# Attention and experts on one core: the second maximum item behind one round with V, routing in four places, and down's product ahead of gate and up

## The chip, the cores and the metric

One core of a Trainium2 chip runs the whole program. The metric is the device time of one execution in microseconds (us), the median of the runs. The engines are PE (TensorE; PEld is its weight loading), ACT (ScalarE), DVE (VectorE), POOL (GpSimd) and SP (SyncE, which issues DMAs here). Each works its own queue in the order of the program and meets the others by semaphores.

## The reference

Two layers over x of shape (2, 2048, 128), float32, each with a residual and a layer norm:

```python
# attention: 16 query heads, 4 key/value heads of 8, window of 128 to either side
Q = (x @ Wq.T).reshape(B, S, HKV, G, HEAD_DIM); K, V likewise from Wk, Wv
scores = einsum('bskgd,bswkd->bskgw', Q, K_win) * scale   # w: 257 places around s, -inf outside
out = einsum('bskgw,bswkd->bskgd', softmax(scores), V_win).reshape(...) @ Wo.T
x = layernorm(x + out)
# experts: 8, the best 2 of softmax(x @ router); their weights through a softmax again
down = (silu(x @ gating[e]) * (x @ up[e])) @ down[e]       # D 128, F 256
x = layernorm(x + sum over the two experts of weight * down)
```

## The kernel before

**Attention.** The 4096 tokens are 32 tiles of 128. Step s (from -2) works on three tiles at once, in five items each: the maximum items A0 to A4 of tile s+2 (`a_item`, matmuls L715, L719, L727, L730, whose maxima DVE takes in `largest_score`, L1328 and L1332), the probability items B0 to B4 of tile s (`b_item`, L754, L745, L766; ACT makes their exponentials, L1056), and V for tile s-1 in rounds of up to two items (`values(t, n)`, L790: round 0 at the end of step t, rounds 1 and 2 early in step t+1). Items use three pairs of PSUM banks in turn, in the order A0 B0 A1 B1 A2 B2 A3 B3 A4 B4, so an item waits until the one three places ahead of it is read (`wait_pair`). The rest of a step on PE: `maxima` (L796), the turned row tile for the router (`turn`, L814), `sums` (L803, of the copy `po` that ACT makes of V's result), in some steps a projection (L848, L850, L841), `logits` (L819) or `ranks` (L828, L831), and `output` (L809). DVE's step is the five reductions, with the reciprocal (L1375) and `attT` (L1378) between the third and the fourth, the residual (L1390) and its statistics (L1397). In between stand the routing operations: `rt_op` (21 for eight tiles: the two best experts and their weights) at three places of a step by `RT_AT`, `slot_op` (8: the row of the expert's region to which a token goes) in one piece by `SLOT_AT`, and `table_op` (19: which block of rows belongs to which expert) by `TABLE_0` and `TABLE_AT`. POOL makes the norm (`norm`, 12 small operations, then x1, L629) and writes the rows sorted by expert to memory (`sort_rows`, L647).

**Experts.** 44 units k of two blocks of 128 rows, in three parts: units 0 to 19 (tiles 0 to 15), 20 to 35 (16 to 27), 36 to 43 (28 to 31). A unit goes through `turn_rows` (PE, transposes of its rows, L945), `round_rows` (ACT, xh, L1111), `rest_rows` (DVE, xl, L1415), `gate_up` (PE, two value loads from the table, which give the expert's column, then six matmuls, L962 to L964), `silu` (ACT, L1118), `hidden` (DVE, L1421), `turn_hidden` (PE, L973), `hidden_out` (ACT, copy from PSUM, L1124), `down` (PE, L982) and `rows_made` (ACT, copy L1130 and the DMA to ys, L1133). The engines' loops over k:

```python
# PE: the steps of MOE_STEPS, then        # ACT: the steps, then
turn_rows(k + 1)                          round_rows(k + 1)
gate_up(k)        # waits xl_done k+1     silu(k)            # waits g_psum k+1
turn_hidden(k-1)  # waits h_done k        hidden_out(k-1)    # waits hT_psum k
down(k-2)         # waits hT_done k-1     rows_made(k-2)     # waits d_psum k-1
```

`turn_rows(k+1)` waits for the rows' DMA and for `xl_done` k+1, that is for `rest_rows(k)`. Steps 32 to 45 (the end of the last tile's attention, its norm, and the last tiles' routing) are put in between: `MOE_STEPS` gives step 32 to unit 0, 33 to 1, 34 to 3, 35 to 4 and so on to 45 in unit 14.

**The end.** POOL gathers each token's two result rows (`rows_back`, L659, 64 gathers in one row of work). Those of a part start when all ys of that part are written (`rows_done`). DVE adds them to x1 (`combine`, L1433) and takes the norm's factors for sets of tiles (`SETS`), ACT scales (L1138), SP writes the output.

Of the kernel before, what the change touches and what calls it, by code (L numbers as in the profile page):

```python
# [10 lines left out]
I32 = mybir.dt.int32  # L11
# [9 lines left out]
NT = TOK // P  # L21
# [38 lines left out]

SETS = [(0, TPS)] + [(t, t + 4) for t in range(TPS, NT, 4)]
CB_TILE, CB_SET = 4, 12
# [11 lines left out]
def part_of(t):  # L74
    return next(ph for ph, (a, b) in enumerate(PARTS) if a <= t < b)
# [121 lines left out]

RT_AT, RANK_AT, SLOT_AT = {}, {}, {}
for m_ in range(NT // RT_TILES):
    s_ = 8 * m_ + 15  # L200
    if m_ < NT // RT_TILES - 2:
        RT_AT.update({s_: (m_, (0, 2), (2, 4), (4, 6)), s_ + 1: (m_, (6, 11), (11, 12), (12, 13)),
                      s_ + 2: (m_, (13, 18), (18, 20), (20, 21))})
        RANK_AT[s_ + 2] = m_
        SLOT_AT[s_ + 3] = m_
    else:
        last_ = m_ == NT // RT_TILES - 1
        RT_AT.update({s_: (m_, (0, 2), (2, 2), (2, 2)), s_ + 1: (m_, (2, 7), (7, 7), (7, 7)),
                      s_ + 2: (m_, (7, 12), (12, 12), (12, 12)), s_ + 3: (m_, (12, 18), (18, 18), (18, 18)),
                      s_ + 4: (m_, (18, 21), (21, 21), (21, 21))} if last_ else  # L210
                     {s_: (m_, (0, 2), (2, 9), (9, 18)), s_ + 1: (m_, (18, 18), (18, 21), (21, 21))})
        RANK_AT[s_ + 1 + 3 * last_] = m_
        SLOT_AT[s_ + 2 + 3 * last_] = m_
RANK_AT[8 * (NT // RT_TILES) + 12] = len(RANKED) - 1
SLOT_AT[8 * (NT // RT_TILES) + 13] = len(RANKED) - 1

# [38 lines left out]
def attention_moe(nc, x, xT, wq, wk, wv, wo, wr, wgu, wd, consts, out, q_scr, xs, ys):  # L255
    with ExitStack() as ctx:
# [193 lines left out]
        def _(sp):  # L450
# [38 lines left out]
            def step(s):  # L489
# [21 lines left out]
                if s in (15, 17, 19):  # L511
                    zeros_last((s - 15) // 2)
                if s == 27:
                    zeros_behind(0, 0, E)
# [45 lines left out]
        def _(pool):  # L560
# [102 lines left out]
            def step(s):  # L663
                if projected(s) is not None:
                    project(*projected(s))
                if s == 28:
                    for t in range(12, 16):
# [7 lines left out]
                if s == 27:  # L675
                    for t in range(8, 12):
                        sort_rows(t)
# [3 lines left out]
            for k in range(NU):  # L681
                if k in MOE_STEPS:
                    step(MOE_STEPS[k])
                if 2 <= k < 10:
                    sort_rows(14 + k)
                if 14 <= k < 18:
                    sort_rows(2 * k - 4)
                    sort_rows(2 * k - 3)
            for t in range(NT):
# [3 lines left out]
        def _(pe):  # L693
# [172 lines left out]
            def step(s):  # L866
# [21 lines left out]

                a_item(s + 2, 1)
                b_item(s, 1)  # L890
# [97 lines left out]
            for k in range(NU):  # L988
                if k in MOE_STEPS:
                    step(MOE_STEPS[k])  # L990
# [12 lines left out]
        def _(act):  # L1003
# [138 lines left out]
            for k in range(NU):  # L1142
                if k in MOE_STEPS:
                    step(MOE_STEPS[k])
# [7 lines left out]
                if k and k in MOE_STEPS:  # L1152
                    routing_exps(MOE_STEPS[k])
            hidden_out(NU - 1)
# [6 lines left out]
        def _(dve):  # L1161
# [174 lines left out]
            def negated(t):  # L1336
                parts = 1 if last_of_batch(t) else 2
                dve.wait_ge(a_max, COUNT["A", t, a_items(t)[-1]])
                if t >= 2:
# [3 lines left out]
                                  AX.X, ALU.max, negate=True).then_inc(nm_done, 1)  # L1343

            def step(s):
                t, a = s - 1, s + 2
                m, *ops = RT_AT.get(s, (0, (0, 0), (0, 0), (0, 0)))
# [4 lines left out]
                if s in SLOT_AT:  # L1352
                    for n in range(SL_OPS):
                        slot_op(SLOT_AT[s], n)
                for n in range(*TABLE_0.get(s, (0, 0))):
                    if s < 30:
                        table_op(0, n)
                g = ln_group(s)
                if g is not None:
                    y = nw[:, g % 2, 1, :]  # L1360
                    dve.wait_ge(mv_done, 4 * g + 4)
                    if g >= 2:
                        dve.wait_ge(x1_done, 4 * (g - 1))
                    dve.tensor_scalar(nw[:, g % 2, 0, :], mv[:, g % 2, :, 1], EPS, None, ALU.add).then_inc(ln_seed, 1)
                    dve.wait_ge(ln_seed, 2 * g + 1)
                    dve.tensor_scalar(y.bitcast(I32), nw[:, g % 2, 0, :].bitcast(I32), -0.5, float(RSQRT_SEED),
                                      ALU.mult, ALU.add).then_inc(ln_seed, 1)
                for n in range(*ops[0]):
                    rt_op(m, n)
                largest_score(a, 1)  # L1370
                largest_score(a, 2)
                if 0 <= t < NT:
                    dve.wait_ge(nd_psum, t + 1)
                    wait(dve, att_done, t)
                    dve.reciprocal(rden[:], pV[:, P:2 * P]).then_inc(den_done, 1)  # L1375
                    dve.wait_ge(den_done, t + 1)
                    wait(dve, y_psum, t)
                    dve.tensor_tensor(attT[:], pV[:, 0:P], rden[:], ALU.mult).then_inc(att_done, 1)  # L1378
                largest_score(a, 3)
                largest_score(a, 4)  # L1380
                if 0 <= a < NT:
                    negated(a)
                for n in range(*TABLE_0.get(s, (0, 0))):
                    if s >= 30:
                        table_op(0, n)
# [5 lines left out]
                for n in range(*ops[1]):  # L1391
                    rt_op(m, n)
                if 0 <= t < NT:
# [4 lines left out]
                for n in range(*ops[2]):  # L1398
                    rt_op(m, n)

# [62 lines left out]
            for k in range(NU):  # L1463
                if k == 0:
                    step(MOE_STEPS[k])
                if k + 1 < NU:
                    rest_rows(k + 1)
                hidden(k)
                if k and k in MOE_STEPS:
                    step(MOE_STEPS[k])  # L1470
# [89 lines left out]
```

## Time and profile before

| | |
|---|---|
| median of three runs | 575.82 us (570.12 to 578.64) |
| profiled execution | 575.41 us, its span 573.8 us |
| mean granted clock of PE | 0.924 |
| busy, share of the span | PE 483.0 us, 84%; PEld 52%; DVE 363.3 us, 63%; ACT 301.1 us, 52%; POOL 241.3 us, 42% |
| attention, steps to the last reciprocal but one | until about 368 us |
| expert units, gate's first matmul of unit 0 to down of unit 43 | 375.7 to 543.8 us |
| last gather issued, end of the span | 562.9 and 573.8 us |

A span is the time from the first to the last instruction; about 1.6 us of the execution lie around it. A matmul's end is modelled. In a timeline line, what stands in brackets is how long the engine was idle before it, and what released it; "issue" is time for which the profile shows no wait. A matmul of 512 columns in the experts' part (L962 to L964) takes 0.39 us in the records at full clock and 0.63 at the lower.

### The profile page before, as it was taken

How to read it: one execution, taken by the hardware profiler on the slowest of the kernel's cores; microseconds unless marked ns; L12 is line 12 of the kernel's file. 1: busy time of each engine (PE TensorE's matmuls, PEld its weight loads, DVE VectorE, ACT ScalarE, POOL GpSimd, SP SyncE). 2: the span in 40 equal slices, each digit the busy share in tenths (PEclk: the TensorE clock that was granted, in tenths of full speed). 3: DMA queues.
4: the chain of work that ended last, by engine and by line, in shares of the span. 5: the costliest groups of instructions: out<-in, count | busy, mean ns of one | idle time of the engine just before them, and what ended most of it. 6: DMA issues, size and time to landing. Idle time of an engine off the chain costs nothing.

```text
span 573.8 us, 12084 instructions
## 1 busy us (share of the span) xinstructions
PE 483.0 (84%) x3865; PEld 296.8 (52%) x3865; DVE 363.3 (63%) x825; ACT 301.1 (52%) x516; POOL 241.3 (42%) x329
## 2 busy tenths in 40 slices
PE   4399899899999999999998988977978899999700
PEld 3264345445454454445454444456867788888500
DVE  1366567778676496668688677652354645677784
ACT  2125455566556455466566466732575555555462
POOL 2131051752532232232746763007701727754772
PEclk9999798999999797799999799967998999999955
DMA  6343116126207225215205130111421445542362
GB/s 164 58 75 72 29 48 149 29 49 148 40 12 174 40 66 121 34 43 121 53 18 83 54 88 21 39 46 47 133 79 54 138 141 159 135 124 71 91 168 59
DMA packets 83948, 46.93 MB, mean 82 GB/s; under 512 B 40496, under 2 KB 79408, under 8 KB 83120
## 3 DMA queue, kind: packets, MB, share of 16 engines
q1 hardware_dynamic: 65216, 31.04, 24.4%
q0 software_dynamic: 4096, 8.40, 5.4%
q10 hardware_dynamic: 14576, 6.72, 4.3%
q8 instruction: 34, 0.56, 0.4%
q14 instruction: 26, 0.21, 0.1%
HBM read 26.47 MB, written 19.40 MB: 80 GB/s over the span
## 4 chain that ended last, share of the span: by engine, by line
PE 57%; DVE 17%; issue 10%; DMA 6%; SPq 3%; POOL 3%; ACT 3%; ACTq 0%; POOLq 0%; DVEq 0%
PE pV L790 12%; DVE mp L1328 7%; PE pX L982 6%; PE pX L962 5%; PE pX L715 5%; PE pX L964 4%; PE pX L963 4%; DMA xt<-xT 3%; DVE rden L1375 3%; PE pX L754 3%; PE pV L973 3%; PE pM L809 2%; PE pX L766 2%; PE pX L745 2%; SPq L435 2%
## 5 line engine op out<-in xcount | busy, mean ns | idle before, releaser
L1328 DVE TENSOR_REDUCE mp<-pX 128x4 f32<-128x1024 f32 (+4 forms) x128 | 149.1, 1187 | 84.4 <-PE pX L719 68.2
L1056 ACT ACTIVATE probs<-pX 128x1024 f32<-128x1024 f32 x152 | 152.6, 1023 | 91.3 <-PE pX L745 75.9
L790 PE MATMUL pV<-probs,vx 128*32 128x512 f32 (+1 forms) x736 | 90.7, 591 | 0.0
L647 POOL DMA_INDIRECT xs<-xr,slot x64 | 63.0, 985 | 44.6 <-DVE ends L1248 26.2
L659 POOL DMA_INDIRECT probs<-ys,source x64 | 64.0, 1001 | 38.1 <-issue 35.4
L715 PE MATMUL pX<-kx,q 48*128 48x512 f32 (+4 forms) x256 | 61.4, 479 | 9.4 <-DMA q<-q_scr 9.4
L754 PE MATMUL pX<-q,kx 50*128 50x512 f32 x248 | 63.0, 505 | 2.5 <-DVE mp L1328 2.0
L1421 DVE TENSOR_TENSOR probs<-probs,pX 128x512 f32<-128x512 f32 x44 | 30.3, 688 | 43.0 <-ACT probs L1118 43.0
L715 PEld LDWEIGHTS pX<-kx,q 48*128 48x128 f32 x256 | 26.2, 203 | 47.7 <-issue 36.1
L962 PE MATMUL pX<-we,qh 128*128 x88 | 41.0, 466 | 11.6 <-issue 9.5
L982 PE MATMUL pX<-we,probs 128*128 x352 | 47.6, 279 | 0.7 <-ACT vx L1130 0.7
L1118 ACT ACTIVATE probs<-pX 128x512 f32<-128x512 f32 x44 | 26.3, 597 | 37.4 <-PE pX L964 37.4
L982 PEld LDWEIGHTS pX<-we,probs 128*128 128x128 f32 x352 | 43.6, 195 | 1.0 <-issue 1.0
L586 POOL CAST kh<-ks 128x512 fp32r<-128x512 f32 x7 | 4.3, 610 | 81.5 <-ACT ks L1033 81.5
L963 PE MATMUL pX<-we,qh 128*128 x88 | 36.5, 415 | 0.0
L964 PE MATMUL pX<-we,ql 128*128 x88 | 36.4, 413 | 0.0
L1415 DVE TENSOR_TENSOR ql<-pX,qh 128x256 fp32r<-128x256 f32 x44 | 18.6, 422 | 26.4 <-ACT qh L1111 25.0
L754 PEld LDWEIGHTS pX<-q,kx 50*128 50x128 f32 x248 | 25.8, 205 | 15.5 <-issue 7.9
L599 POOL CAST qh<-qs 128x512 fp32r<-128x512 f32 x7 | 4.3, 610 | 69.9 <-ACT qs L1036 69.9
L1375 DVE RECIPROCAL rden<-pV 128x128 f32<-128x128 f32 x32 | 30.3, 948 | 4.8 <-PE pV L803 4.8
L790 PEld LDWEIGHTS pV<-probs,vx 128*32 128x32 f32 x736 | 18.0, 114 | 27.5 <-issue 21.4
L745 PE MATMUL pX<-mask 64*128 64x256 bf16 (+1 forms) x184 | 31.9, 343 | 0.0
(151 smaller groups left out, 832.5 us busy)
## 6 DMA issues: line engine op xcount, KB each, us to landing
q<-q_scr SPq DMA_DIRECT2D x46, 128.0 KB, 4.3
xt<-xs SPq DMA_DIRECT2D x88, 64.0 KB
ys<-vx ACTq DMA_DIRECT2D x44, 128.0 KB, 1.9
xt<-xT SPq DMA_DIRECT2D x8, 512.0 KB, 5.9
q_scr<-qh SPq DMA_DIRECT2D x32, 64.0 KB
q<-stage SPq DMA_DIRECT2D x128, 2.0 KB
xr<-x SPq DMA_DIRECT2D x8, 256.0 KB, 6.4
raw<-wgu SPq DMA_DIRECT2D x4, 512.0 KB, 5.7
```

Source lines behind the costliest of these rows:

```text
L647: pool.indirect_dma_start(xs[ph][:, :], bass.IndirectOffsetOnAxis(ap=slot[:, t, k:k + 1], axis=0), tile(t), None, bounds_check=ROWS - 1, o ...
L659: pool.indirect_dma_start(yin[:, t % YIN, k, :], None, ys[ph][:, :], bass.IndirectOffsetOnAxis(ap=source[:, t, k:k + 1], axis=0), bounds_c ...
L715: mm = pe.matmul(bank[:, pr, 0:64 * (k1 - k0)], q_cols(t, KA, pr, i, i + 1), k_cols(KA, pr, k0, k1), start=True, stop=True, skip_group_che ...
L754: mm = pe.matmul(bank[:, pr, :], k_cols(KB, pr, k0, k0 + 2), q_cols(t, KB, pr, 0, 4), start=True, stop=True, skip_group_check=True)
L790: mm = pe.matmul(pV[row:row + 32, cols], vx[:, chunk, pr, :], src[:, pr, cols], start=n == 0, stop=True, skip_group_check=True)
L962: pe.matmul(to, xh[:, k % 2, rows], hi, start=True, stop=False, skip_group_check=True)
L963: pe.matmul(to, xh[:, k % 2, rows], lo, start=False, stop=False, skip_group_check=True)
L964: mm = pe.matmul(to, xl[:, k % 2, rows], hi, start=False, stop=True, skip_group_check=True)
L982: mm = pe.matmul(pX[2][:, 1, h * D:(h + 1) * D], hidT[:, k % 2, at:at + P], we[:].bitcast(F32)[:, bass.ds(expert[k, h] + 4 * F + f * D, D) ...
L1056: act.activation(dst, src[:], ACT.Exp).then_inc(exp_done, 1)
L1328: dve.tensor_reduce(mp[:, t % 2, 0, :, i, :], src[:, :, 0:2 * n].rearrange("p r (c v k) -> p r v c k", v=NV, k=32), AX.XY, ALU.max).then_i ...
L1375: dve.reciprocal(rden[:], pV[:, P:2 * P]).then_inc(den_done, 1)
```

## The change

On PE, A1 goes ahead of V's round 2 and of the maxima. Routing and slot operations are spread over four places of DVE's step, slots over two steps, and the norm's seeds of step 33 stand ahead of them. Steps 34 and 35 go to unit 4, 36 and 37 to unit 5, 38 to 45 to units 6 to 13. Rank matmuls, sorts and tables are shifted to fit. In a unit `down(k-2)` stands ahead of `gate_up(k)` on PE and `rows_made(k-2)` ahead of `silu(k)` on ACT. In DVE's step `seeds(g)` and `routing(place)` are helpers around the old operations. `combine` starts one unit sooner, and the first set for the last norm has 20 tiles instead of 16.

```diff
-SETS = [(0, TPS)] + [(t, t + 4) for t in range(TPS, NT, 4)]
+SETS = [(0, 20), (20, 24), (24, 28), (28, 32)]
...
     if m_ < NT // RT_TILES - 2:
-        RT_AT.update({s_: (m_, (0, 2), (2, 4), (4, 6)), s_ + 1: (m_, (6, 11), (11, 12), (12, 13)),
-                      s_ + 2: (m_, (13, 18), (18, 20), (20, 21))})
-        RANK_AT[s_ + 2] = m_
-        SLOT_AT[s_ + 3] = m_
+        RT_AT.update({s_: (m_, (0, 2), (2, 2), (2, 2), (2, 5)), s_ + 1: (m_, (5, 7), (7, 8), (8, 11), (11, 13)),
+                      s_ + 2: (m_, (13, 15), (15, 15), (15, 18), (18, 21))})
+        RANK_AT[s_ + 3] = m_
+        SLOTS_AT.update({s_ + 3: (m_, (0, 0), (0, 0), (0, 0), (0, 3)), s_ + 4: (m_, (3, 5), (5, 6), (6, 8), (8, 8))})
...
-        TABLE_0 = {27: (0, 5), 30: (5, 13), 31: (13, TB_OPS)}
+        TABLE_0 = {30: (0, 9), 31: (9, TB_OPS)}
...
-        TABLE_AT = (14, 18)
+        TABLE_AT = (13, 18)
...
-            COMBINE_AT.append(max([LAST_UNIT[part_of(t)] + 6] + [n + 1 for n in COMBINE_AT[-1:]]))
-        MOE_STEPS = {k: NT + i for i, k in enumerate((0, 1, 3, 4, 5, 6, 7, 8, 9, 10, 11, 12, 13, 14))}
+            COMBINE_AT.append(max([LAST_UNIT[part_of(t)] + 5] + [n + 1 for n in COMBINE_AT[-1:]]))
+        MOE_STEPS = {0: [NT], 1: [NT + 1], 4: [NT + 2, NT + 3], 5: [NT + 4, NT + 5]}
+        MOE_STEPS.update({k: [NT + k] for k in range(6, 14)})
...
@@ -873,7 +874,10 @@
                 if has(s - 1):
-                    for n in range(1, len(rounds(s - 1))):
+                    values(s - 1, 1)
+                a_item(s + 2, 1)
+                if has(s - 1):
+                    for n in range(2, len(rounds(s - 1))):
                         values(s - 1, n)
...
-                a_item(s + 2, 1)
                 b_item(s, 1)
                 a_item(s + 2, 2)
...
@@ -986,15 +989,15 @@
                     turn_rows(k + 1)
+                if k >= 2:
+                    down(k - 2)
                 if k:
                     gate_up(k)
                     turn_hidden(k - 1)
-                if k >= 2:
-                    down(k - 2)
...
@@ -1140,17 +1143,17 @@
                     round_rows(k + 1)
+                if k >= 2:
+                    rows_made(k - 2)
                 silu(k)
                 if k:
                     hidden_out(k - 1)
-                if k >= 2:
-                    rows_made(k - 2)
...
@@ -1342,32 +1345,40 @@
+                if g is not None and s > NT:
+                    seeds(g)
+                routing(0)
                 largest_score(a, 1)
+                if g is not None and s <= NT:
+                    seeds(g)
+                routing(1)
                 largest_score(a, 2)
...
                     dve.tensor_tensor(attT[:], pV[:, 0:P], rden[:], ALU.mult).then_inc(att_done, 1)
+                routing(2)
                 largest_score(a, 3)
...
                     dve.bn_stats(st6[:, t % 4, :], tile(t)).then_inc(st_done, 1)
+                routing(3)
```

## Rows read from the trace of the kernel before

**Rows 1.** timeline, steps 6 and 7: start us, us, engine, line, operation [idle before <-releaser]
```profile
104.90 1.50 PE L790 MATMUL pV<-probs,vx 128*32 128x512 f32 x16
...
106.72 0.49 PE L715 MATMUL pX<-kx,q 48*128 48x512 f32 x2
...
107.30 2.36 DVE L1328 TENSOR_REDUCE mp<-pX 128x4 f32<-128x1024 f32 x2 [1.42 <-PE pX L719]
...
107.65 0.21 PE L719 MATMUL pX<-mask 64*128 64x64 bf16 x2
...
109.57 0.95 DVE L1375 RECIPROCAL rden<-pV 128x128 f32<-128x128 f32 x1
...
112.03 0.50 PE L766 MATMUL pX<-q,kx 50*128 50x256 f32 x4 [1.08 <-DVE mp L1328]
...
119.71 0.95 DVE L1375 RECIPROCAL rden<-pV 128x128 f32<-128x128 f32 x1
```
**Rows 2.** waits over the whole span: us in total, times, longest us
```profile
PE pX L962 <- issue: 9.5, 19, 1.1
...
PE pX L766 <- DVE mp L1328: 8.2, 17, 1.1
```
**Rows 3.** busy time by stretch: PE, PEld, DVE, ACT, POOL, granted clock, DMA, GB/s
```profile
461.10:527.00 65.90, 64.06 (x409) 54.56 (x408) 41.51 (x116) 37.13 (x82) 36.34 (x37) 1.00 0.46 126
...
394.00:401.00 7.00, 7.00 (x30) 6.27 (x30) 1.11 (x2) 2.00 (x5) 5.62 (x7) 0.51 0.21 60
```
**Rows 4.** timeline, expert unit 37
```profile
516.05 0.49 PE L962 MATMUL pX<-we,qh 128*128 x1
...
517.99 1.06 PE L982 MATMUL pX<-we,probs 128*128 x8
...
518.24 0.58 ACT L1124 COPY probs<-pV 128x512 f32<-128x512 f32 x1
...
518.88 0.38 PE L945 MATMUL pX<-cst,xt 128*128 128x128 f32 x2
```
**Rows 5.** timeline, expert unit 16
```profile
445.31 0.41 DVE L1415 TENSOR_TENSOR ql<-pX,qh 128x256 fp32r<-128x256 f32 x1
...
445.88 0.41 PE L945 MATMUL pX<-cst,xt 128*128 128x128 f32 x2
...
447.42 0.49 PE L962 MATMUL pX<-we,qh 128*128 x1 [1.14 <-issue]
```
**Rows 6.** timeline, expert units 23 and 24
```profile
471.19 0.49 PE L962 MATMUL pX<-we,qh 128*128 x1 [0.23 <-issue]
...
472.05 0.42 DVE L1415 TENSOR_TENSOR ql<-pX,qh 128x256 fp32r<-128x256 f32 x1 [1.28 <-ACT qh L1111]
...
474.15 0.50 PE L962 MATMUL pX<-we,qh 128*128 x1
```
**Rows 7.** timeline, GpSimd's gathers: first of the last 32, of the last 8
```profile
522.36 0.99 POOL L659 DMA_INDIRECT probs<-ys,source  x1 [9.90 <-issue]
...
553.75 1.00 POOL L659 DMA_INDIRECT probs<-ys,source  x1 [0.30 <-issue]
```
**Rows 8.** timeline, expert unit 43: gate's first matmul and down's last eight
```profile
537.18 0.50 PE L962 MATMUL pX<-we,qh 128*128 x1
...
542.64 1.15 PE L982 MATMUL pX<-we,probs 128*128 x8 [0.65 <-ACT vx L1130]
```
**Rows 9.** timeline, expert units 2 and 3
```profile
385.89 0.58 ACT L1124 COPY probs<-pV 128x512 f32<-128x512 f32 x1 [0.26 <-PE pV L973]
...
385.93 0.78 PE L962 MATMUL pX<-we,qh 128*128 x1
...
392.89 0.30 PE L814 MATMUL pM<-cst,xr 128*128 128x128 f32 x1 [3.43 <-POOL xr L629]
```
**Rows 10.** timeline, expert unit 12, at the lower clock
```profile
431.60 0.79 PE L962 MATMUL pX<-we,qh 128*128 x1 [1.14 <-issue]
...
435.27 0.58 ACT L1124 COPY probs<-pV 128x512 f32<-128x512 f32 x1
```

More of the change, by code:

```diff
@@ L512, in step @@
                     zeros_last((s - 15) // 2)
-                if s == 27:
+                if s == 28:
                     zeros_behind(0, 0, E)
@@ L666, in step @@
                 if s == 28:
-                    for t in range(12, 16):
+                    for t in range(8, 12):
                         sort_rows(t)
@@ L674, in step @@
                     sort_rows(s - 20)
-                if s == 27:
-                    for t in range(8, 12):
+                if s == 29:
+                    for t in range(12, 16):
                         sort_rows(t)
@@ L681, in _ @@
             for k in range(NU):
-                if k in MOE_STEPS:
-                    step(MOE_STEPS[k])
+                for s in MOE_STEPS.get(k, ()):
+                    step(s)
                 if 2 <= k < 10:
                     sort_rows(14 + k)
-                if 14 <= k < 18:
-                    sort_rows(2 * k - 4)
-                    sort_rows(2 * k - 3)
+                if 13 <= k < 17:
+                    sort_rows(2 * k - 2)
+                    sort_rows(2 * k - 1)
             for t in range(NT):
@@ L988, in _ @@
             for k in range(NU):
-                if k in MOE_STEPS:
-                    step(MOE_STEPS[k])
+                for s in MOE_STEPS.get(k, ()):
+                    step(s)
                 if k + 1 < NU:
                     turn_rows(k + 1)
+                if k >= 2:
+                    down(k - 2)
                 if k:
@@ L1142, in _ @@
             for k in range(NU):
-                if k in MOE_STEPS:
-                    step(MOE_STEPS[k])
+                for s in MOE_STEPS.get(k, ()):
+                    step(s)
                 if k + 1 < NU:
                     round_rows(k + 1)
+                if k >= 2:
+                    rows_made(k - 2)
                 silu(k)
@@ L1149, in _ @@
                     hidden_out(k - 1)
-                if k >= 2:
-                    rows_made(k - 2)
-                if k and k in MOE_STEPS:
-                    routing_exps(MOE_STEPS[k])
+                    for s in MOE_STEPS.get(k, ()):
+                        routing_exps(s)
             hidden_out(NU - 1)
@@ L1343, in negated, with seeds, routing @@
                                   AX.X, ALU.max, negate=True).then_inc(nm_done, 1)
+            def seeds(g):
+                y = nw[:, g % 2, 1, :]
+                dve.wait_ge(mv_done, 4 * g + 4)
+                if g >= 2:
+                    dve.wait_ge(x1_done, 4 * (g - 1))
+                dve.tensor_scalar(nw[:, g % 2, 0, :], mv[:, g % 2, :, 1], EPS, None, ALU.add).then_inc(ln_seed, 1)
+                dve.wait_ge(ln_seed, 2 * g + 1)
+                dve.tensor_scalar(y.bitcast(I32), nw[:, g % 2, 0, :].bitcast(I32), -0.5, float(RSQRT_SEED),
+                                  ALU.mult, ALU.add).then_inc(ln_seed, 1)
             def step(s):
                 t, a = s - 1, s + 2
-                m, *ops = RT_AT.get(s, (0, (0, 0), (0, 0), (0, 0)))
+                nothing = (0, (0, 0), (0, 0), (0, 0), (0, 0))
+                m, *ops = RT_AT.get(s, nothing)
+                r, *ranked = SLOTS_AT.get(s, nothing)
+                def routing(place):
+                    for n in range(*ops[place]):
+                        rt_op(m, n)
+                    for n in range(*ranked[place]):
+                        slot_op(r, n)
+                g = ln_group(s)
                 largest_score(a, 0)
@@ L1351, in step @@
                     dve.bn_aggr(mv[:, ((t - 1) // 4) % 2, (t - 1) % 4, :], st6[:, (t - 1) % 4, :]).then_inc(mv_done, 1)
[L1352 to L1369, printed above, removed]
+                if g is not None and s > NT:
+                    seeds(g)
+                routing(0)
                 largest_score(a, 1)
+                if g is not None and s <= NT:
+                    seeds(g)
+                routing(1)
                 largest_score(a, 2)
@@ L1390, in step @@
                     dve.tensor_tensor(tile(t), pM[:, 256:384], tile(t), ALU.add).then_inc(z_done, 1)
-                for n in range(*ops[1]):
-                    rt_op(m, n)
-                if 0 <= t < NT:
                     if t >= 4:
@@ L1397, in step @@
                     dve.bn_stats(st6[:, t % 4, :], tile(t)).then_inc(st_done, 1)
-                for n in range(*ops[2]):
-                    rt_op(m, n)
+                routing(3)
             dve.wait_ge(q_split, 1)
@@ L1464, in _ @@
                 if k == 0:
-                    step(MOE_STEPS[k])
+                    step(NT)
                 if k + 1 < NU:
@@ L1468, in _ @@
                 hidden(k)
-                if k and k in MOE_STEPS:
-                    step(MOE_STEPS[k])
+                if k:
+                    for s in MOE_STEPS.get(k, ()):
+                        step(s)
                 for ph in range(1, NPH):
```

21 lines of the change are left out of this document (10 added, 11 removed).

## The prediction

> **What bounds the kernel now.** I read the page first: PE is busy 84% of a span of 573.8 us (the page's table above), and no other engine reaches 64%. A share is an average, so each stage was then read by itself in the timeline.
>
> *Attention, 32 steps.* A settled step lasts 10.13 us: one reciprocal starts at 109.57, the next at 119.71 [rows 1]. It is one loop through two engines. PE lands the second maximum item (L715 at 106.72), DVE reduces it and the third (2.36 us), takes the reciprocal, reduces the fourth; only then may PE start the last probability item (L766, behind a wait of 1.08 us for DVE). From there PE runs on through V's round 0, the next step's first items, V's rounds 1 and 2 and the maxima, and lands the next second item. Steps that also carry a projection or logits use that slack: over all steps L766 waits for DVE only 8.2 us [rows 2].
>
> *Experts, 44 units of two blocks.* From 461.1 to 527 PE is busy 64.06 of 65.9 us at the full granted clock [rows 3]. PE's order in unit k is rows turned for k+1 (T), gate and up of k (G), hidden turned for k-1 (H), down of k-2 (D). In unit 37 G starts at 516.05, D at 517.99, T at 518.88 [rows 4]. From G of unit 24 at 474.15 to that of unit 37 the mean unit is 41.9 / 13 = 3.22 us, and 2.96 us, G of unit 23 at 471.19 to G of unit 24 at 474.15, is PE's own work without a gap [rows 6]. The rest comes with the pair of value loads in front of G, which are instructions of PE's queue. In unit 16 DVE finishes xl at 445.31 + 0.41 = 445.72, T starts at 445.88, and G only at 447.42: 1.54 us from T to G on an empty array, 1.70 us from xl [rows 5]. I formed this distance for all units from 2 to 43: it is never under 1.66 us and in half of them within 0.1 us of that. Units 23 and 24 show it again: 472.05 + 0.42 = 472.47 to 474.15 is 1.68 us [rows 6]. So PE's queue doesn't reach the value loads while T's wait for xl is open, and from its release to G there is a fixed 1.7 us.
>
> *The end.* GpSimd gathers 64 times in a row, 1.30 us each. The last 32 start at 522.36, when the result of unit 35 is in memory; the eight of the last part, from 553.75 on, need unit 43 [rows 7]. Unit 43's D starts at 542.64 [rows 8], some 7 us before it is needed. So today unit 35 sets the end, and the units behind it are covered by the gathers.
>
> **The change, part by part.**
>
> *Second maximum item ahead of V's last round.* It moves A1 ahead of V's round 2 and the maxima. Rounds 1 and 2, maxima and x1's turn take 104.90 to 106.72, 1.82 us together; round 2 and the two small ones are about 1.1 us of it [rows 1]. DVE then reduces A1 in its present idle time, and the chain starts from the third item instead, which lands where it did. Before, DVE began the third reduction when half of 2.36 us was over, at 108.48; the item had landed with L719's end, 107.65 + 0.21 = 107.86. So the loop shortens by 0.62 us, to about 9.5 us. Where PE's own work is the bound (projections, logits), only the present wait of L766 can be won, 0.2 to 0.3 us. Five steps (2, 6, 25, 27, 28) have the full wait: 5 x 0.62 = 3.1 us; the others bring what is left of the 8.2 us, some 2.9 us. Sum 6.0 us. V's round 2, the copy of the output and the maxima end 0.4 to 0.5 us later; the copy's follower (sums) stands behind A2 anyway.
>
> *Routing in four places.* The same operations of about 0.2 us. Some now stand between A1 and A2 and behind the reciprocal, on DVE's chain, three or four per step in some six steps: 0 to 3 us; I take 1. Attention together: -5 us (-9 to -1).
>
> *Later units for steps 34 to 37, seeds first.* PE stood 3.43 us in unit 3 for GpSimd's norm (L814 at 392.89) [rows 9]. A unit later this wait is gone. It is not booked separately: below, units are counted at their new length, which replaces it.
>
> *D ahead of G, result copy ahead of SiLU.* Here is the cost. D(k-2) needs the copy of hidden rows of k-2 (L1124). That copy needs H(k-2), which stands at the end of unit k-1, and on ACT it stands behind SiLU(k-1), which needs G(k-1). Before, a whole unit lay between copy and D. Now only T does. In unit 37 G starts at 516.05 and the copy ends at 518.24 + 0.58 = 518.82: 2.77 us behind G's start [rows 4], the same in every unit at full clock. D cannot start sooner, and behind D in PE's queue stand the value loads for G(k). So a unit costs 2.77 us, then the release to G. With T in between that release costs 1.68; with D's eight matmuls instead of T's two, somewhat more. Bound: G of unit 23 starts at 471.19 behind a gap, and by 472.47 PE's queue has already passed 6 + 4 + 8 matmuls [rows 6], 1.28 us or at most 0.07 each, so six more cost at most 0.43. A unit is between 2.77 + 1.66 = 4.43 and 2.77 + 1.68 + 0.43 = 4.88 us. I take 4.7, against 3.22 now. ACT and DVE have about 2.0 and 1.4 us of work in a unit and don't bind.
>
> *Extras of early units.* Unit 4 carries steps 34 and 35: logits wait for x1T's copy, which stands behind the hidden copy on ACT, +1.6; unit 5 +0.5; the second logits +0.3; the two exponentials with table loads between SiLUs +2.9. Together 5.3 us (2 to 8).
>
> *Combine one unit sooner, sets of 20.* Twelve operations of 0.2 us leave the tail of DVE; they lie beside gathers: 0.
>
> **The sum**, against the profiled run (span 573.8, 1.6 around it: 575.4; the median of the three is 575.8). G of unit 2 starts at 385.93. Attention takes 5 off; D(0) waits for the copy that ends at 385.89 + 0.58 = 386.47 [rows 9], so G(2) moves to 386.47 + 1.68 + 0.25 = 388.4, less 5 is 383.4. 41 units at 4.7 are 192.7, extras 5.3: G(43) starts at 581.4. From G(43) to D(43) is 542.64 - 537.18 = 5.46 [rows 8]: 586.9. From D(35) at 517.99 to the gather at 522.36 are 4.37 [rows 4, 7]: the last eight gathers start at 591.2. Unit 35 would let them start sooner: G(36) at 548.5, D(35) at 551.5, gathers from 555.9, 24 x 1.30 later is 587.1. So the end passes from GpSimd to PE. From the first of the eight gathers to the end of the span is 573.8 - 553.75 = 20.05: 611.3, and with 1.6 around it **613 us**.
>
> One rule of the Trainium skill speaks against this working. The page Perfetto Trace Analysis, section Per-engine timelines, has a matmul wait in a queue of its own while the sequencer already decodes what follows; by it the value loads would run while D waits. The trace does not agree for T's wait (never under 1.66 us); whether it holds for D's no row shows. By the rule it would be rival 1.
>
> **Rivals.**
>
> 1. *D's wait holds back D, not the value loads.* Then a unit is 2.77, 0.24 (as from the copy to D at the end) and D's 0.89 (517.99 to 518.88, where T follows): 3.9 us. G(2) 382.6, G(36) 520.5, D(35) 523.5, gathers from 527.9, and 51.4 us more: 579.3, **581 us**. For it: some waits may travel with their matmul. Against: rows 5 and 6.
>
> 2. *The granted clock falls in the new gaps.* PE would work 2.96 of 4.7 us. At the lower level (1.2 GHz) unit 12 had 4.25 us from G to the end of the copy (431.60 to 435.27 + 0.58) [rows 10], against 2.77: +1.5 us a unit, **674 us** if all 41 ran so, 643 for half. For it: after PE's 3.43 us of standing, 394 to 401 ran at 0.51 [rows 3, 9]. Against: the new gaps are each near 1 us, and unit 16 with its 1.14 us stayed at full clock [rows 5].
>
> 3. *Faster: the value loads' 9.5 us of idle time before G [rows 2] vanish and D finds its copy ready.* With it 3.4 us of the norm wait, 5 of attention, 2 as D(35) comes earlier in its unit: 575.4 - 19.9 = **555 us**. It decides where the copy ends before T does, within about 2.0 us of G's start; the rows say 2.77, and nothing in the change brings SiLU or H forward. Only if ACT's copy needed no H could it be.
>
> **Chances.** Forecast (unit of 4.4 to 4.9 us, clock mostly full) 0.67, its own range 597 to 622; rival 1 and mixtures with it (575 to 597) 0.12; rival 2 (622 to 674) 0.16; rival 3 0.05. The range 588 to 640 takes in the bounds of the unit's length (41 x 0.27 down, 41 x 0.18 up), of attention and extras, part of rival 1 and the half of rival 2, and leaves out some 0.2. Two per cent, about what can be told from no change here, is 564 to 587: faster 0.05, within 0.07, slower 0.88.
>
> **What the profile would show.** Right: steps of 9.5 us where no projection is, 9.9 otherwise; no 3.4 us wait at L814; in the units D directly behind T, starting 0.05 to 0.25 us behind the end of L1124; about 0.8 us of PE idle before L982 and 1 us or more before L962; unit length 4.7; the last eight gathers waiting for ys. Wrong: D starting within 2 us of G (the reading of the order is false), or no idle before L962 (rival 1), or L962 at 0.63 us instead of 0.40 through the units (rival 2).

## The result and the profile after

The changed kernel takes 639.61 us, median of four runs (630.02 to 645.32); the kernel before, on the same chip, 573.88 us (570.12 to 578.64). The ratio is 1.107, with a 95% interval of 1.098 to 1.117. Here and below a ratio isn't that of the medians, because every kernel has quicker and slower executions and only the quicker are compared (630.02 and 636.78 us of the four here); one execution of a later kernel, which took 670.2 us at a mean granted clock of 0.62, is left out in the same way. The profiled execution is the quickest of the four, 630.02 us with a span of 628.4, so the sum of 613 us, made against one profiled execution, is to be held against 630.0 first, and the median stands another 9.6 us above it.

TensorE now stands still for a part of every unit. The two rows that carry this in the page of the changed kernel are PE's busy tenths in 40 slices and the granted clock beside them:

```profile
PE   3599999999989799899998977776777777776720
...
PEclk8559899999999879999968895999999999999965
```

From slice 26 on PE is at 7 where the kernel before had 9, and the clock did not fall. The windows of the changed kernel (columns as in rows 3) put a number on it:

```profile
450.00:500.00 50.00, 36.03 (x209) 28.62 (x208) 19.94 (x66) 17.31 (x41) 22.20 (x23) 1.00 0.39 111
500.00:550.00 50.00, 35.54 (x208) 28.14 (x207) 21.00 (x58) 18.49 (x43) 25.39 (x26) 1.00 0.34 88
```

PE is busy 36.0 and 35.5 of 50 us at a granted clock of 1.00, against 64.06 of 65.9 before [rows 3]. Two units of the changed kernel, PE's timeline and then ScalarE's (line numbers are three higher than before in these functions: gate and up L965 to L967, hidden turned L976, rows turned L948, down L985, hidden copy L1127):

```profile
473.97 0.49 PE L965 MATMUL pX<-we,qh 128*128 x1 [0.76 <-issue]
...
475.46 0.60 PE L976 MATMUL pV<-cst,probs 128*128 128x128 f32 x4
475.89 0.38 PE L948 MATMUL pX<-cst,xt 128*128 128x128 f32 x2
476.87 1.15 PE L985 MATMUL pX<-we,probs 128*128 x8 [0.59 <-ACT probs L1127]
478.77 0.49 PE L965 MATMUL pX<-we,qh 128*128 x1 [0.75 <-DVE ql L1422]
```
```profile
475.66 0.60 ACT L1121 ACTIVATE probs<-pX 128x512 f32<-128x512 f32 x1 [2.04 <-PE pX L967]
476.15 0.58 ACT L1127 COPY probs<-pV 128x512 f32<-128x512 f32 x1
```

This is the chain of the prediction, read off (G is the start of gate and up, D of down, T of the turned rows, as there): G starts at 473.97, the copy ends at 476.15 + 0.58 = 476.73, 2.76 us later (rows 4 had 2.77), D starts 0.14 us behind it, and the next G at 478.77, 1.90 us behind D. The unit is 4.80 us; over units 5 to 42 it is 4.80 to 4.96 and 4.86 in the mean, save two of 5.36 that carry later steps.

The waits of the changed kernel's TensorE (us in total, times, longest), which answer to rows 2:

```profile
PE pX L985 <- ACT probs L1127: 23.3, 39, 0.9
PE pX L965 <- DVE ql L1422: 22.5, 28, 0.9
PE pX L965 <- issue: 12.6, 16, 0.9
...
PE pX L767 <- DVE mp L1331: 7.3, 8, 1.8
...
PE pX L948 <- DMA xt<-xs: 3.9, 1, 3.9
```

Two gaps a unit, one before D (23.3 us) and one before G (22.5 + 12.6 = 35.1 us), where before there was one of 9.5 us [rows 2]. The gap before G is put down to DVE's ql for most units, though the ql that G needs has long been done: T, which stands ahead of D, waits for the same one (`xl_done` k+1), and the ql that ends shortly before G is the next unit's. Wherever it ends, G follows D by 1.83 to 2.06 us in all units from 2 on. It is the value loads, as the experiments show. The 3.9 us for unit 0's rows is new, and was not in the prediction. (L948 and L767 are three and one higher than L945 and L766 before.)

### The profile page after: what moved, and what is told of

It reads as the page before. It is cut to its first block, busy times and chain, and to the rows that moved or that the text cites. A ratio compares the mean times of both kernels' runs of the same rounds, so it can differ in the third digit from the quotient of the medians.

```text
span 628.4 us, 12072 instructions
## 1 busy us (share of the span) xinstructions
PE 494.0 (79%) x3865; PEld 293.2 (47%) x3865; DVE 364.6 (58%) x813; ACT 295.4 (47%) x516; POOL 241.8 (38%) x329
## 3 DMA queue, kind: packets, MB, share of 16 engines
q1 hardware_dynamic: 65216, 31.04, 22.5%
## 4 chain that ended last, share of the span: by engine, by line
PE 51%; DVE 17%; issue 12%; ACT 8%; DMA 7%; SPq 4%; POOL 1%; ACTq 0%; DVEq 0%; POOLq 0%
PE pV L791 12%; PE pX L965 5%; PE pX L716 5%; DMA xt<-xT 4%; PE pX L755 4%; DVE xr L1440 4%; PE pX L967 3%; PE pX L966 3%; ACT probs L1121 3%; PE pX L985 2%; ACT probs L1059 2%; DVE mp L1331 2%; PE pM L810 2%; SPq L435 2%; DVE ql L1422 2%
## 5 line engine op out<-in xcount | busy, mean ns | idle before, releaser
L1331 DVE TENSOR_REDUCE mp<-pX 128x4 f32<-128x1024 f32 (+4 forms) x128 | 151.7, 1189 | 81.0 <-PE pX L720 65.0
L791 PE MATMUL pV<-probs,vx 128*32 128x512 f32 (+1 forms) x736 | 95.0, 587 | 0.0
L985 PE MATMUL pX<-we,probs 128*128 x352 | 50.7, 287 | 23.9 <-ACT probs L1127 23.3
L965 PE MATMUL pX<-we,qh 128*128 x88 | 40.2, 457 | 35.1 <-DVE ql L1422 22.5
L985 PEld LDWEIGHTS pX<-we,probs 128*128 128x128 f32 x352 | 42.8, 191 | 33.5 <-issue 33.4
L965 PEld LDWEIGHTS pX<-we,qh 128*128 128x128 f32 x88 | 16.9, 192 | 45.8 <-issue 43.7
L1133 ACT COPY vx<-pX 128x256 f32<-128x256 f32 x44 | 16.4, 373 | 42.6 <-PE pX L985 42.6
L966 PE MATMUL pX<-we,qh 128*128 x88 | 35.6, 405 | 0.0
L967 PE MATMUL pX<-we,ql 128*128 x88 | 35.5, 403 | 0.0
L1066 ACT COPY po<-pV 128x512 f32<-128x512 f32 x32 | 18.8, 586 | 33.4 <-PE pV L791 33.4
```

Of the source, the lines that this page charges most:

```text
L791: mm = pe.matmul(pV[row:row + 32, cols], vx[:, chunk, pr, :], src[:, pr, cols], start=n == 0, stop=True, skip_group_check=True)
L965: pe.matmul(to, xh[:, k % 2, rows], hi, start=True, stop=False, skip_group_check=True)
L966: pe.matmul(to, xh[:, k % 2, rows], lo, start=False, stop=False, skip_group_check=True)
L967: mm = pe.matmul(to, xl[:, k % 2, rows], hi, start=False, stop=True, skip_group_check=True)
L985: mm = pe.matmul(pX[2][:, 1, h * D:(h + 1) * D], hidT[:, k % 2, at:at + P], we[:].bitcast(F32)[:, bass.ds(expert[k, h] + 4 * F + f * D, D) ...
L1331: dve.tensor_reduce(mp[:, t % 2, 0, :, i, :], src[:, :, 0:2 * n].rearrange("p r (c v k) -> p r v c k", v=NV, k=32), AX.XY, ALU.max).then_i ...
```

## The experiments

Each ratio is to runs of the kernel before on the same chip. The runs fell on four chips, which the text names where it matters.

**The order alone.** The kernel before with only the two orders moved:

```diff
-                if k:
-                    gate_up(k)
-                    turn_hidden(k - 1)
                 if k >= 2:
                     down(k - 2)
+                if k:
+                    gate_up(k)
+                    turn_hidden(k - 1)
```

and rows_made(k - 2) ahead of silu(k) on ScalarE.

> The kernel before with one part of the change alone: down(k-2) ahead of gate_up(k) on PE, rows_made(k-2) ahead of silu(k) on ACT. Theory (down waits for the copy of its hidden rows, and the value loads wait behind down): units of 4.8 to 4.95 us from unit 2 on, the end set by unit 43, 618 to 632 us, so nearly all of the changed kernel's loss. Rival (much of the loss is in attention, the start of the experts or the later steps of routing): units shorter than that and under 600 us.

Measured: 625.4 us against 574.0, ratio 1.097 (1.086 to 1.108). Its settled units are 4.80 to 4.96 us. The order of down is nine tenths of the loss by the ratios. Counted in the profiles from G of unit 0 to the end of the span, which leaves attention out, it is all of it: 198.1 us before, 254.2 with the order alone, 249.2 with the whole change.

**The order undone**, everything else of the change kept (the reverse of that diff).

> The changed kernel with that one part undone on both engines; all the rest of the change stays. Theory: units back to a mean of 3.2 us, the end again set by unit 35 and the gathers, 565 to 578 us; what the rest of the change brings or costs can be read from it. By my prediction's terms for attention (-5) and for the norm wait (-3.4) it would be 566 us; if the wait for the rows of unit 0 (3.85 us) and the half-clock stretches at the end of attention belong to the change, about 573. Rival (the rest costs as well): over 585.

Measured: 582.4 us, ratio 1.013 (1.005 to 1.022), with settled units of 3.0 to 3.5 us, 3.21 in the mean of units 24 to 37. From G of unit 0 to the end it takes 199.6 us, as the kernel before. So the rest of the change doesn't pay for itself either: a gain was expected, and it costs about one per cent here, ahead of the units. The experiments on attention below look into that.

**The value loads ahead of down's wait**, all else as in the changed kernel:

```diff
+            def loads(k):      # tb_ops wait and the two value loads, taken out of gate_up
...
+                if k:
+                    loads(k)
                 if k >= 2:
                     down(k - 2)
...
                 if k:
                     gate_up(k)
```

> The changed kernel with the two value loads of unit k ahead of down(k-2) instead of behind it; nothing else differs. Theory (the loads are held up behind down's wait): a unit is 2.77 to the copy's end, 0.14 to down, 0.9 of down and little more, 3.9 to 4.0 us, and the time falls to 585 to 597 us. Rival (the loads cost nothing, down or ACT's order is what lengthens the unit): still 4.8 us and 630 us.

Measured: 598.8 us, ratio 1.050 (1.034 to 1.067). The medians differ from the changed kernel's by 41 us, the profiled spans by 35 (593.5 against 628.4), and as much from G of unit 2 to G of unit 43 (167.2 against 202.2), with nothing else moved. PE's timeline of this kernel, one unit:

```profile
498.85 1.16 PE L989 MATMUL pX<-we,probs 128*128 x8 [0.60 <-ACT probs L1133]
499.76 0.48 PE L969 MATMUL pX<-we,qh 128*128 x1
...
502.66 1.15 PE L989 MATMUL pX<-we,probs 128*128 x8 [0.60 <-ACT probs L1133]
503.57 0.48 PE L969 MATMUL pX<-we,qh 128*128 x1
```

The wait before D is what it was (0.60 us); the one before G is gone, and G follows D by 0.91 us instead of 1.90. The unit is 3.81 us, which is rival 1's 3.9. So the loss of 1.64 us a unit (3.22 to 4.86) splits: 1.05 us is the loads standing bare behind the wait, and 0.59 us remains when they do not.

**The same loads moved in the kernel before**, a unit ahead:

```diff
...
+                if k == 0:
+                    loads(1)
                 if k:
                     gate_up(k)
+                    if k + 1 < NU:
+                        loads(k + 1)
                     turn_hidden(k - 1)
```

> The kernel before with the value loads of unit k+1 right behind gate_up(k), a unit ahead. Theory (before, 1.5 us of loads stand between the turned rows and gate and up, in a loop of two units of 6.5 us): the idle time before gate's first matmul falls from 9.5 us to near 0, units of 2.95 to 3.05 us, gathers of the second part 7 to 9 us sooner, 565 to 569 us. Rival (the loads are hidden today, PE is the bound): no change, 572 to 576 us.

Measured: 560.0 us, ratio 0.982 (0.970 to 0.995), and again on another chip, as the base of two later runs:

> The kernel before with the loads of unit k+1 behind gate_up(k), the same kernel as the fourth run, here as the base for the next two. Again 0.975 to 0.99 of before on a chip whose code arrives in time (units of 2.96 us); on one with long stalls of all engines, as in the last four runs, nearer 0.99.

Measured: 560.2 us against 572.0, ratio 0.976 (0.970 to 0.983). The windows of the first of the two:

```profile
460.00:500.00 40.00, 40.00 (x269) 35.42 (x269) 28.16 (x75) 24.29 (x55) 30.13 (x31) 1.00 0.57 152
```

PE busy 40.00 of 40 us, and units of 2.96 us, which is PE's own work [rows 6]. This is the quickest kernel of the study, and quicker than the 565 to 569 us expected.

**Twice as many value loads** in the changed kernel, to have their price by itself:

```diff
+                    pe.value_load(tab[0:1, ph, 1, i:i + 1], min_val=0, max_val=(E - 1) * EW)
                     expert[k, h] = pe.value_load(tab[0:1, ph, 1, i:i + 1], min_val=0, max_val=(E - 1) * EW)
```

> The changed kernel with each unit's two value loads issued twice (the first result of each pair is dropped), still behind the wait of down; nothing else differs. It measures the disputed price itself. Theory (TensorE issues nothing behind a wait, so the loads lie bare between down and gate_up): the changed kernel's units of 4.86 us and the 3.81 us of the kernel with the loads ahead put two loads at 1.05 us, so units of 5.7 to 6.1 us, the whole 670 to 690 us. Rival (most of the 1.05 us is something else, register moves or a refill behind the wait): units of 5.0 to 5.3 us, 640 to 655 us.

Its whole time, 810.1 us, can't be read against the changed kernel's: this run fell on a chip on which the kernel before takes 695.9 us. The unit can. PE's timeline at full clock:

```profile
569.97 1.15 PE L986 MATMUL pX<-we,probs 128*128 x8 [0.59 <-ACT probs L1128]
573.43 0.49 PE L966 MATMUL pX<-we,qh 128*128 x1 [2.31 <-issue]
```

The idle time before G is 2.31 us, not 0.75: two loads more cost 1.56 us, and the unit is 6.37 us (567.06 to 573.43), above both theories' figures. (Every third unit or so of this run falls to the lower clock and takes 7.8 us.) The wait before D is again 0.59. So a pair of loads takes about 1.55 us of TensorE's queue; in the changed kernel 1.05 us of it lies bare. That the rest, some 0.5 us, lies beside down's matmuls, which would still run when the queue is past them, is the difference of the two figures and isn't shown by itself. My expectation had taken the bare part for the whole.

**The A1 move alone** in the kernel before (on the chip of 695.9 us), and then with the loads ahead (on the chip of 572.0 us, beside the second run of the loads alone):

```diff
                 if has(s - 1):
-                    for n in range(1, len(rounds(s - 1))):
+                    values(s - 1, 1)
+                a_item(s + 2, 1)
+                if has(s - 1):
+                    for n in range(2, len(rounds(s - 1))):
                         values(s - 1, n)
...
-                a_item(s + 2, 1)
                 b_item(s, 1)
```

> The kernel before with one edit, the second maximum item (A1) put behind the first further round with V instead of behind the wo product. Theory (the 8.2 us wait of line 766 on the maxima is what the move removes, and TensorE sets the steps): full-clock steps of 10.13 us become 9.9 us, some 24 of them, so 3 to 5 us less, 569 to 572 us. Rival (what the move saves is paid back in granted clock, since TensorE is busier): G(0) no earlier, 573 to 577 us. Rival (the shorter steps of the changed kernel come from the routing in four places): steps stay at 10.13 us, 574 us.

Measured: 685.1 us, ratio 0.987 (0.979 to 0.996). The times expected can't be judged on this chip; the settled steps are 9.93 us, so it is the A1 move that shortens them.

> The kernel before with the loads ahead and the A1 move. Theory (A1 is worth the 0.2 us a step that the last four runs showed at full clock, 9.9 against 10.1): 3 to 5 us under the run beside it, ratio to before 0.965 to 0.98. Rival (it is paid back in granted clock): within 1 us of the run beside it.

Measured: 563.7 us, ratio 0.986 (0.980 to 0.993), beside 0.976 (0.970 to 0.983) for the loads alone. This is neither expectation: the median is 3.5 us above the run beside it. There is no gain, and the intervals overlap, so a loss isn't shown either. The steps did shorten: from 10.13 us to 9.93 us between two settled reciprocals of this kernel (TensorE's wait on the maxima, on line 766 in both, fell from 8.4 to 4.4 us). TensorE's waits from 50 to 370 us, first without and then with the move:

```profile
PE pX L766 <- DVE mp L1336: 8.4, 17, 1.1
PE pX L727 <- ACT probs L1064: 8.4, 20, 0.6
```
```profile
PE pX L727 <- ACT probs L1066: 9.8, 26, 0.5
PE pX L766 <- DVE mp L1338: 4.4, 7, 0.8
```

**The rest without A1**: the order undone, A1 undone (again the chip of 695.9 us).

> The kernel with the order of down undone (582.4 us) and the A1 move undone as well: routing in four places, later tables, scatters and zeros, and the sets of 20 tiles remain. If the routing in four places is what costs, it stays at 580 to 586 us; if the A1 move is what costs through the clock, it falls to 572 to 577 us. The wait of about 3.9 us for unit 0's rows should be there in both.

Measured: 685.5 us, ratio 0.989 (0.984 to 0.994). This chip's times can't be set against the 572 to 586 us of the expectation. The wait for unit 0's rows is there, but of 1.7 us. TensorE waits 10.4 us for the maxima, against 8.2 us in the kernel before (on a quick chip).

**The rows of unit 0 earlier**: the order undone, and

```diff
-        TABLE_0 = {30: (0, 9), 31: (9, TB_OPS)}
+        TABLE_0 = {27: (0, 5), 30: (5, 13), 31: (13, TB_OPS)}
...
                 if s == 28:
-                    for t in range(8, 12):
+                    for t in range(8, 16):
                         sort_rows(t)
...
-                if s == 29:
-                    for t in range(12, 16):
-                        sort_rows(t)
```

> The kernel with the order of down undone (582.4 us), with tables 0 at their old steps (27, 30, 31) and the scatters of tiles 12 to 15 in step 28 instead of 29. Theory (unit 0's rows are late because table and scatters are): the 3.9 to 4.1 us wait of line 948 for xt goes, G(0) is 3.5 to 4 us earlier, 577 to 579 us. Rival (the time goes to something else late at the same place, the copies or the maxima): under 1 us, 581 to 583 us.

Measured: 683.5 us, ratio 0.987 (0.979 to 0.995). The wait for xt in front of unit 0, 4.1 us with the order undone, isn't among its waits, and the last step of attention is 7.8 us where it was 11.3. So the two edits remove the wait. They weren't taken apart, so which of them, table or scatters, held the rows longer isn't shown; and the whole time on this chip doesn't resolve 4 us.

**All of it, without the two losses.** Order undone, loads ahead, unit 0's rows early:

> The changed kernel with the order of down undone, the loads of unit k+1 behind gate_up(k), and unit 0's tables and scatters early again: all of the change but its order of units, without the two losses found so far. Theory (routing in four places gives nothing beside A1, and costs where the clock is low): 0 to 4 us above the kernel with A1 and loads ahead. Rival (it was the late rows alone that cost): equal to it or up to 3 us below.

Measured: 566.4 us, ratio 0.989 (0.981 to 0.997), 2.7 us above the kernel with A1 and the loads, with intervals that overlap. And the same with A1 undone (on a chip on which the kernel before takes 574.6 us):

> The last kernel (all of the change but its order of units, loads ahead, unit 0's tables and scatters early) with the A1 move undone as well. Theory (the A1 move shortens full-clock steps by 0.2 us and is paid back, with more, in low clock: G(0) at 367 to 376 us without it, at 379 to 385 us with it): steps of 10.1 us at full clock, G(0) at 369 to 375 us, the whole 556 to 561 us, ratio to before 0.97 to 0.985. Rival (the four places cost the clock too): G(0) at 378 to 382 us, 563 to 568 us as with A1.

Measured: 576.4 us, ratio 1.011 (1.0005 to 1.022). Both theories were missed: without A1 the kernel is slower against its base, not quicker (the two ratios come from two chips), and gate's first matmul of unit 0 starts at 396.77, the latest of all. The windows from 50 to 370 us of four kernels with the loads ahead, in this order: nothing else changed, A1, A1 and the rest, the rest without A1:

```profile
50.00:370.00 320.00, 294.99 (x2792) 149.39 (x2790) 231.81 (x430) 187.80 (x271) 129.18 (x200) 0.95 0.30 66
```
```profile
50.00:370.00 320.00, 303.21 (x2707) 148.43 (x2705) 228.00 (x399) 178.76 (x261) 129.55 (x200) 0.90 0.30 64
```
```profile
50.00:370.00 320.00, 299.43 (x2727) 147.54 (x2731) 231.09 (x405) 181.41 (x263) 129.63 (x200) 0.93 0.30 64
```
```profile
50.00:370.00 320.00, 292.27 (x2567) 143.88 (x2566) 216.23 (x380) 171.36 (x245) 119.99 (x181) 0.88 0.30 62
```

The granted clock falls from 0.95 to 0.90, 0.93 and 0.88, and the matmuls and weight loads done by 370 us go with it (the count behind each x). Unit 0's G starts at 371.6, 382.1, 380.2 and 396.8 us. The idle time differs less: 25.0 us of the 320 in the first and 27.7 in the last. The four are single executions of 561.5, 568.5, 565.3 and 580.5 us, and the second and the last were the slowest of their kernels' six, so the four clocks can't be put down to the edits.

What the edits do to the waits can be read, as it is far steadier. In the same four kernels TensorE waits for the maxima 8.4, 4.4, 7.3 and 12.9 us. The last:

```profile
PE pX L764 <- DVE mp L1335: 12.9, 18, 2.0
```

So the A1 move takes 4.0 us of this wait away, and the rest of the change puts 2.9 us back beside it (4.5 us without it). It is one profile each, but the changed kernel and the two from it that keep its attention have the same 7.3 us, and the kernels with the attention of before 8.2 to 8.6.

## Why the prediction came out as it did

**The number: inside the range by luck.** The median of 639.6 us lies 0.4 us under the upper end of 588 to 640, and outside the 597 to 622 that the forecast gave its own mechanism. The range reached so far only to take in half of rival 2, the lower clock in the units, and that did not come. Profile against profile the loss is 54.6 us (575.4 to 630.0), where 37.6 were forecast. The mechanism was right; the sum fell short by 17 us, of which 9.8 came up to G of unit 2 (attention and the first two units), 4.2 in the units from there to unit 43, and 3.2 in the tail.

**Right: the place, the chain and the sign.** Each link of it stands in the rows above: D waits for the copy of its own hidden rows, which ends 2.77 us behind G in every unit from 2 to 43 but one (unit 11, 3.20); the loads are behind that wait and run bare; gaps of 0.8 us before D's weight loads (0.6 before its matmuls) and again before G; the norm's 3.43 us wait of rows 9 is gone; the end passed from GpSimd's gathers behind unit 35 to TensorE's unit 43. The last eight gathers waited for unit 43's rows (below). The order alone made a ratio of 1.097 of the 1.107, and moving only the loads took 35 us back.

**The unit: 4.7 forecast, 4.86 measured.** The bound from both sides (4.43 to 4.88) held, but I chose too low in it. The term that was too small is the way from the release to G: 1.68 + 0.25 = 1.93 us taken, 0.14 + 1.95 = 2.09 measured. In the prediction's terms, the 0.25 us for D's eight matmuls in the place of T's two was 0.41, just under the bound of 0.43. The doubled loads fit: the pair costs 1.55 us of the queue, so some 0.5 us of the 2.09 is left for what stands ahead of it. With 41 units that is 6.6 us; the extras of units 4 to 12 were then smaller than the 5.3 us booked (about 3), so that the stretch from unit 2 to unit 43 came out 4.2 us over.

**Attention: a gain of 5 us forecast, a loss of 3.5 measured in the profile.** This was the term that failed most. G of unit 0 was to start near 370.7 and started at 379.2, 8.5 us late, half of the 17.1 us between 611.3 and 628.4. (Another 1.3 us went between unit 0 and unit 2.) Three things are in it.

- The waits. I expected 9.5 us from a loop that loses 0.62 us, and 6.0 us of the wait on the maxima gone. The settled step is 9.8 to 9.9, and the wait went only from 8.2 to 7.3 us. The A1 move by itself took 4.0 us of it, and the rest of the change, the routing in four places with it, put 2.9 us back, where I had taken 1 (of 0 to 3). The wait of the last maximum item (A4) for ScalarE, L727 before and L728 after, also grew: 8.9 us over all steps before, 9.5 after, in 25 steps instead of 21. That a second loop, through ScalarE, stood 0.3 us behind the one I had found would fit; no run tests it.
- Unit 0's rows, 3.85 us. I had put the later tables and scatters at nothing. The edit leaves the operations that write table 0's rows to step 31; in the kernel before they were in step 30. PE's timeline of the changed kernel:

```profile
369.81 0.61 PE L791 MATMUL pV<-probs,vx 128*32 128x512 f32 x4
374.27 0.64 PE L948 MATMUL pX<-cst,xt 128*128 128x128 f32 x2 [3.85 <-DMA xt<-xs]
```

  The rows' transfers are issued at 371.81 instead of 366.17, as the table's rows end at 369.88 instead of 365.30 and the last scatter is issued at 368.66. The prediction didn't follow who waits for what was moved. With both put back the wait went.
- The granted clock. In the profiled runs on chips of 572 to 575 us, G of unit 0 starts at 375.7, 367.4, 369.7 and 371.6 us with the attention of before, and at 379.2, 385.5, 380.8, 382.1, 380.2 and 396.8 with any part of the new one. Three of these six have the wait of 3.9 to 4.1 us; without it the six are still at 375 to 397. One profile stands for each, three of the six (385.5, 382.1 and 396.8) are of the slowest execution of their kernel, and without those and the wait it is 375.3 to 380.2 against 367.4 to 375.7. So the share of the clock, and that of each edit, isn't settled.

**The tail: 20.05 forecast, 23.3 measured.** The first of the last eight gathers started at 605.12, 4.5 us behind D(43) as forecast (4.4). It waited for the rows of unit 43, although the profile names DVE: it stands 2.88 us behind the issue of these rows (602.24), as the gather behind unit 35 did before (519.48 to 522.36). The buffer that it needs is that of tile 12, 16 tiles back, and DVE had combined that tile at 564.34. The timeline of the changed kernel, ScalarE's issue of the rows, GpSimd's first of the last eight and its last, then DVE's combine four tiles ahead of the end:

```profile
602.24 0.37 ACTq L1136 DMA_DIRECT2D ys<-vx  x1
...
605.12 0.99 POOL L660 DMA_INDIRECT probs<-ys,source  x1 [5.21 <-DVE xr L1440]
...
614.22 1.00 POOL L660 DMA_INDIRECT probs<-ys,source  x1 [0.30 <-issue]
...
616.66 0.74 DVE L1440 SCALAR_TENSOR_TENSOR xr<-probs,wts,xr 128x128 f32<-128x128 f32 x2
```

And the kernel before, the same issue for unit 35:

```profile
519.48 0.37 ACTq L1133 DMA_DIRECT2D ys<-vx  x1
```

A group of four tiles takes DVE 7.13 us (609.53 to 616.66), factors included, and a group's gathers 8 x 1.30 = 10.4. Before, DVE waited for gathers (1.36 us before the last tile); now it comes out of the units with twelve tiles to combine, works on them from 602.15 on without a gap, and the end is its own. The set of 20 tiles isn't the cause: the order alone, with the old sets, has 24.05 us (597.55 to 621.6). The plan combines a tile a unit, so longer units push the combine back, and that I had booked at 0.

**The rivals.** Rival 1 was false for this kernel and true for the one with the loads ahead (3.9 forecast, 3.81 measured). The Trainium skill (page Perfetto Trace Analysis, section Per-engine timelines) has a matmul's wait stand in a queue of its own while the sequencer goes on to decode. At down's wait the trace doesn't show this: 1.90 us from D to G with the loads behind the wait and 0.91 with them ahead. But the kernel writes this wait as a statement of its own (`pe.wait_ge`) ahead of matmuls whose addresses come from registers, and no run shows whether the matmul carries it; so the rule may hold and not apply here. The whole kernel with the loads ahead took 595.1 us in its profiled execution, not rival 1's 581, as attention gained nothing there either and early units took longer than 3.9. Rival 2 was false: L965 took 0.40 to 0.49 us, and the clock stood at 1.00 from 400 to 600 us. It wasn't far off, though: with the loads doubled, on the chip of 695.9 us, the clock does fall again and again, here with PE busy 12.20 of 20 us:

```profile
560.00:580.00 20.00, 12.20 (x61) 9.62 (x60) 5.76 (x20) 5.28 (x12) 4.28 (x5) 0.88 0.20 56
```

Rival 3 named the right prize, the 9.5 us of loads before G, but it was to be had by moving the loads, not down.

**What stays open.** Whether the A1 move and the rest of the change (the routing in four places above all) each lower the clock in attention. On the chip of 695.9 us each alone was one per cent quicker than the kernel before (0.987 and 0.989); on the chips of 572 and 574.6 us A1 gave nothing beside the loads ahead, and the rest alone, though helped by loads ahead and early rows, was one per cent slower. Together they gave 0.989. The waits for the maxima (12.9 us for the rest alone, 7.3 for both) go this way, but they don't explain the chip of 695.9 us.

## What to carry to other kernels

When a consumer is moved ahead in an engine's queue, count three things: how long its producer's chain is now, which scalar loads stand behind its wait, and what they cost bare. Register loads that an in-order engine needs for its next item belong ahead of the last thing that waits; here that one line was worth 2% where the reordering lost 10%. A table or scatter that is moved "later, into idle time" has a first consumer: find it before booking the move at zero.

## What was not expected of the hardware

- A pair of value loads on TensorE with what goes with it takes about 1.55 us of its queue (the idle time before gate goes from 0.75 to 2.31 us with two loads more), as long as the six matmuls of gate and up of a unit (473.97 to 475.46).
- The same kernel before took 572 to 575 us on three chips and 695.9 us on a fourth. There TensorE, ScalarE and DVE stood still together while GpSimd's gathers went on, TensorE for 6 to 14 us at a time in the three kernels with the old order of units, and up to 27 us with the loads doubled. The A1 kernel's timeline on that chip:

```profile
639.26 1.09 PE L975 MATMUL pV<-cst,probs 128*128 128x128 f32 x4 [8.30 <-issue]
...
652.56 0.37 ACT L1132 COPY vx<-pX 128x256 f32<-128x256 f32 x1 [13.44 <-remote]
...
653.17 2.07 PE L984 MATMUL pX<-we,probs 128*128 x8 [12.82 <-ACT vx L1132]
```

  The pauses came at unit 15 or 16, at unit 25 and at unit 41 in all three kernels with the old order, and in other places in one or two of them; the chain of their pages puts 10 to 14% of the span on another core or an unknown queue. What they are no run shows; that code arrives late there, as an expectation above takes for granted, is a guess. Ratios taken there are diluted by them.
- Gaps of 0.6 to 0.8 us twice in 4.86 us left the granted clock at 1.00 from 400 to 600 us. In attention, with PE busy 297.57 of the 320 us from 50 to 370, it averaged 0.94 in the same profile, and 0.88 to 0.96 in the nine others on the quick chips.
